# Another order of the helper calls in a four-engine graph network kernel on Trainium2

## The reference

```python
h = relu(layernorm(x)); A = (adj != 0)
for l in range(3):
    aggr = einsum('bst,bsd->btd', A, h @ weight[l])
    gi, gh = aggr @ w_ih.T + b_ih, h @ w_hh.T + b_hh
    r, z = sigmoid(gi_r + gh_r), sigmoid(gi_z + gh_z)
    h = (1 - z) * tanh(gi_n + r * gh_n) + z * h
x = x + h
hp = relu(layernorm(x)) @ W.T
e = leaky(hp @ a1 [rows] + hp @ a2 [columns], 0.2)
x = x + softmax(where(adj > 0, e, -9e15)) @ hp
```

## Time and profile before

| | us |
|---|---|
| median of 3 runs (498.48 to 499.28) | 499.28 |
| the profiled execution | 499.44 |
| its span, first to last instruction | 497.6 |
| PE, DVE, ACT, POOL busy in the span | 461.2, 442.6, 359.4, 142.5 |
| mean granted TensorE clock | 0.985 |

### The profile page before, as it was taken

How to read it: one execution, slowest core, us unless ns; L and a number is a source line. 1 busy time by engine, 2 the same in 40 slices (tenths; PEclk the granted TensorE clock), 3 DMA queues, 4 the chain that set the end, 5 groups by cost and what they waited for, 6 DMA issues and landing times.

```text
span 497.6 us, 8083 instructions
## 1 busy us (share of the span) xinstructions
PE 461.2 (93%) x2547; PEld 376.5 (76%) x2547; DVE 442.6 (89%) x1087; ACT 359.4 (72%) x641; POOL 142.5 (29%) x170
## 2 busy tenths in 40 slices
PE   5699998999999999999999999999999999998675
PEld 3476776887888878788888878788888888776465
DVE  3869888899999999999999999999999999997854
ACT  3365664786969778796968778795968878677375
POOL 2214244332312333332312333242213333131500
PEclk9989998999999999999999999999999999999979
DMA  6620030020303020030303021030303000000001
GB/s 179 211 85 2 1 105 0 20 89 22 107 21 107 22 86 22 22 106 21 107 23 106 12 69 49 22 106 23 105 22 106 1 24 1 22 1 22 23 1 42
DMA packets 26746, 26.34 MB, mean 53 GB/s; under 512 B 840, under 2 KB 18512, under 8 KB 26704
## 3 DMA queue, kind: packets, MB, share of 16 engines
q1 hardware_dynamic: 26704, 25.83, 16.2%
HBM read 21.63 MB, written 4.19 MB: 52 GB/s over the span
## 4 chain that ended last, share of the span: by engine, by line
PE 45%; DVE 27%; issue 13%; ACT 11%; DMA 2%; POOL 1%; SPq 1%; DVEq 0%; ACTq 0%; POOLq 0%
PE X L1108 12%; DVE prob L838 4%; DVE fresh L774 4%; DVE out_sb L850 4%; PE G L1193 3%; DVE neg_ring L706 3%; ACT e L455 3%; DVE rv L748 2%; PE R L1092 2%; PE R L1093 2%; PE R L1094 2%; PE Z L1092 2%; PE Z L1093 2%; PE G L1215 2%; PE Z L1094 2%
## 5 line engine op out<-in xcount | busy, mean ns | idle before, releaser
L1108 PE MATMUL X<-A_ring,nat_hi 128*128 128x512 f32 x192 | 78.8, 410 | 1.2 <-DVE A_ring L700 1.0
L1108 PE MATMUL X<-A_ring,nat_lo 128*128 128x512 f32 x192 | 76.3, 397 | 0.0
L838 DVE SCALAR_TENSOR_TENSOR prob<-e 128x512 f32<-128x512 f32 x64 | 62.0, 968 | 13.2 <-ACT e L456 13.0
L1226 PE MATMUL G<-hp,probT 128*128 128x128 f32 x512 | 67.3, 275 | 0.7 <-DVE out_sb L850 0.7
L275 POOL TENSOR_TENSOR hT_lo<-hT,hT_hi 128x512 fp32r<-128x512 f32 x19 | 25.4, 1337 | 147.6 <-ACT hT_hi L382 131.5
L1226 PEld LDWEIGHTS G<-hp,probT 128*128 128x128 f32 x512 | 63.2, 192 | 2.1 <-issue 0.9
L455 ACT ACTIVATE e<-g,nb 128x512 f32<-128x512 f32 x64 | 46.6, 729 | 5.6 <-DVE nb L831 5.5
L456 ACT ACTIVATE e<-g,nb 128x512 f32<-128x512 f32 x64 | 45.9, 717 | 0.0
L462 ACT COPY probT<-G 128x512 f32<-128x512 f32 x64 | 37.4, 584 | 10.4 <-PE G L1215 10.3
L432 ACT ACTIVATE gn<-npre,vecs 128x512 f32<-128x512 f32 x48 | 34.6, 720 | 13.7 <-DVE npre L758 13.7
L1108 PEld LDWEIGHTS X<-A_ring,nat_hi 128*128 128x128 f32 x192 | 36.5, 190 | 10.3 <-issue 1.6
(11 more groups left out here) (136 smaller groups left out, 1210.1 us busy)
## 6 DMA issues: line engine op xcount, KB each, us to landing
adj_raw<-in_adj SPq DMA_DIRECT2D x16, 1024.0 KB, 5.6
x_ring<-in_x SPq DMA_DIRECT2D x16, 256.0 KB, 2.9
out_x<-out_sb SPq DMA_DIRECT2D x16, 256.0 KB, 2.2
wih_in<-in_L_gnn_w_ih SPq DMA_DIRECT2D x1, 192.0 KB, 3.1
wl_in<-in_L_gnn_weight SPq DMA_DIRECT2D x1, 192.0 KB, 4.1
whh_in<-in_L_gnn_w_hh SPq DMA_DIRECT2D x1, 192.0 KB, 4.2
w_in<-in_L_gnn_W SPq DMA_DIRECT2D x1, 64.0 KB
vec_in<-in_L_gnn_b_ih SPq DMA_DIRECT2D x1, 1.5 KB
```

The costliest lines, as they stand in the source:

```text
L838: dve.scalar_tensor_tensor(out=prob[:, c], in0=e1[:, c % 2], scalar=1.0, in1=e2[:, c % 2], op0=ALU.mult, op1=ALU.max, accum_out=psums[:, k ...
L1108: mm = pe.matmul(X[:], part[s][:, c], A_ring[:, (k - s) % RING, c], start=(c == 0 and part is nat_hi), stop=(c == C - 1 and part is nat_lo))
L1226: mm = pe.matmul(G2[:, c * D:(c + 1) * D], probT[:, c % 2, j], hp[:, (k + 1) % 2, j, 0:D], start=(j == 0), stop=(j == C - 1))
```

## The change

The helpers and their instructions stay. Their sequence is another in rounds 0 to 3, in the repeated part and in rounds 16 to 19, on PE, ACT, DVE and POOL. The repeated part has its seam in another place: some calls of a round now stand at the head of the next one (`from_state(i - 1, 0, Z)` and `from_neighbours(i - 1, 0, Z)` on PE, `new_state(i - 1, 0)` on DVE, `state_high(i - 1, 1)` on ACT), and the statistics of x and `norm_scale` stand in the round before (`i + 1`). The new sequences, cut; those of before stand in the listing above:

```diff
 POOL
-            def full(i, k):
-                norm_scale(i, k)
-                natural_low0(i, k)
-                scale2(i, k)
-                centre2(i, k)
-                normed2(i, k)
-                state_low(i, k, 1)
+            def full(i):
+                natural_low0(i, i % RING)
+                scale2(i, i % RING)
+                centre2(i, i % RING)
+                normed2(i, i % RING)
+                norm_scale(i + 1, (i + 1) % RING)
+                state_low(i, i % RING, 1)
 ACT
+            def full(i):
+                neighbours_high(i, i % RING, 2)
+                own_candidate(i, i % RING, 2)
+                normed(i, i % RING)
+                state_high(i - 1, (i - 1) % RING, 1)
+                natural_high(i, i % RING, 1)
+                update_gate(i, i % RING, 2)
+                exps(i, i % RING, 0)
+                reset_gate(i, i % RING, 2)
+                neighbours_high(i, i % RING, 1)
+                exps(i, i % RING, 1)
+                turned_prob(i, i % RING, 0)
+                exps(i, i % RING, 2)
+                first_state_high(i, i % RING)
+                candidate(i, i % RING, 2)
+                turned_prob(i, i % RING, 1)
+                first_state(i, i % RING)
+                own_candidate(i, i % RING, 1)
+                exps(i, i % RING, 3)
+                reset_gate(i, i % RING, 1)
+                turned_prob(i, i % RING, 2)
+                neighbours_high(i, i % RING, 0)
+                turned_prob(i, i % RING, 3)
+                update_gate(i, i % RING, 1)
+                candidate(i, i % RING, 1)
+                attention_input(i, i % RING)
+                own_candidate(i, i % RING, 0)
+                reset_gate(i, i % RING, 0)
+                natural_high(i, i % RING, 2)
+                state_high(i, i % RING, 2)
+                values(i, i % RING)
+                update_gate(i, i % RING, 0)
+                candidate(i, i % RING, 0)
 DVE
+            def full(i):
+                new_state(i - 1, (i - 1) % RING, 0)
+                neighbours_low(i, i % RING, 2)
+                scores(i, i % RING)
+                natural_low(i, i % RING, 1)
+                offsets(i, i % RING)
+                adjacency(i, i % RING)
+                probabilities(i, i % RING, 0)
+                reset(i, i % RING, 2)
+                neighbours_low(i, i % RING, 1)
+                probabilities(i, i % RING, 1)
+                keep(i, i % RING, 2)
+                before_tanh(i, i % RING, 2)
+                probabilities(i, i % RING, 2)
+                natural_high0(i, i % RING)
+                residual(i, i % RING)
+                x2_stats(i, i % RING)
+                renew(i, i % RING, 2)
+                x2_mean(i, i % RING)
+                new_state(i, i % RING, 2)
+                state_low(i, i % RING, 0)
+                probabilities(i, i % RING, 3)
+                reset(i, i % RING, 1)
+                before_tanh(i, i % RING, 1)
+                neighbours_low(i, i % RING, 0)
+                x_stats(i + 1, (i + 1) % RING)
+                keep(i, i % RING, 1)
+                renew(i, i % RING, 1)
+                new_state(i, i % RING, 1)
+                output(i, i % RING)
+                mask(i, i % RING)
+                natural_low(i, i % RING, 2)
+                x_mean(i + 1, (i + 1) % RING)
+                reset(i, i % RING, 0)
+                before_tanh(i, i % RING, 0)
+                state_low(i, i % RING, 2)
+                keep(i, i % RING, 0)
+                renew(i, i % RING, 0)
 PE
+            def full(i):
+                from_state(i - 1, (i - 1) % RING, 0, Z)
+                from_neighbours(i - 1, (i - 1) % RING, 0, Z)
+                neighbours(i, i % RING, 2)
+                neighbour_terms(i, i % RING)
+                from_state(i, i % RING, 2, HN)
+                from_state(i, i % RING, 2, R)
+                from_state(i, i % RING, 2, Z)
+                from_neighbours(i, i % RING, 2, R)
+                turn_state(i, i % RING, 1)
+                from_neighbours(i, i % RING, 2, Z)
+                from_neighbours(i, i % RING, 2, IN)
+                turn_result(i, i % RING)
+                neighbours(i, i % RING, 1)
+                from_state(i, i % RING, 1, Z)
+                from_state(i, i % RING, 1, R)
+                turn_prob(i, i % RING, 0)
+                from_state(i, i % RING, 1, HN)
+                from_neighbours(i, i % RING, 1, Z)
+                turn_prob(i, i % RING, 1)
+                turn_input(i, i % RING)
+                attend(i, i % RING, 0)
+                from_neighbours(i, i % RING, 1, IN)
+                from_neighbours(i, i % RING, 1, R)
+                turn_prob(i, i % RING, 2)
+                attend(i, i % RING, 1)
+                neighbours(i, i % RING, 0)
+                turn_prob(i, i % RING, 3)
+                attend(i, i % RING, 2)
+                from_state(i, i % RING, 0, R)
+                from_state(i, i % RING, 0, HN)
+                turn_normed(i, i % RING)
+                attend(i, i % RING, 3)
+                from_neighbours(i, i % RING, 0, R)
+                turn_state(i, i % RING, 2)
+                from_neighbours(i, i % RING, 0, IN)
+                project(i, i % RING)
```

Of the written-out rounds, DVE's first calls and those of round 3, and POOL's of round 3:

```diff
             x_stats(0, 0)
             x_mean(0, 0)
             wl_out()
-            whh_out()
-            vectors_out()
-            natural_high0(0, 0)
-            whh_high()
             adjacency(0, 0)
+            natural_high0(0, 0)
+            x_stats(1, 1)
+            whh_out()
+            whh_high()
...
             neighbours_low(3, 3, 2)
             state_high(2, 2, 1)
-            x_mean(3, 3)
-            residual(3, 3)
             natural_low(3, 3, 1)
+            natural_high0(3, 3)
+            x2_stats(3, 3)
+            x2_mean(3, 3)
             reset(3, 3, 2)
             before_tanh(3, 3, 2)
-            x2_stats(3, 3)
-            x2_mean(3, 3)
             neighbours_low(3, 3, 1)
-            adjacency(3, 3)
-            natural_high0(3, 3)
             keep(3, 3, 2)
...
-            scale2(3, 3)
             natural_low0(3, 3)
             centre2(3, 3)
+            scale2(3, 3)
+            norm_scale(4, 0)
             normed2(3, 3)
```

More of the change, by code:

```diff
@@ L990, in _ @@
             natural_low(3, 3, 2)
+            mask(2, 2)
             keep(3, 3, 0)
@@ L994, in _ @@
             state_high(3, 3, 1)
-            every_graph(full)
+            neighbours_low(4, 0, 2)
+            scores(4, 0)
+            natural_low(4, 0, 1)
+            offsets(4, 0)
+            mask(3, 3)
+            adjacency(4, 0)
+            probabilities(4, 0, 0)
+            reset(4, 0, 2)
+            neighbours_low(4, 0, 1)
+            probabilities(4, 0, 1)
+            keep(4, 0, 2)
+            before_tanh(4, 0, 2)
+            probabilities(4, 0, 2)
+            natural_high0(4, 0)
@@ new lines, in _ @@
+            residual(4, 0)
+            x2_stats(4, 0)
+            renew(4, 0, 2)
+            x2_mean(4, 0)
+            new_state(4, 0, 2)
+            state_low(4, 0, 0)
+            probabilities(4, 0, 3)
+            reset(4, 0, 1)
+            before_tanh(4, 0, 1)
+            neighbours_low(4, 0, 0)
+            x_stats(5, 1)
+            keep(4, 0, 1)
+            renew(4, 0, 1)
+            new_state(4, 0, 1)
+            output(4, 0)
+            mask(4, 0)
+            natural_low(4, 0, 2)
@@ new lines, in _ @@
+            x_mean(5, 1)
+            reset(4, 0, 0)
+            before_tanh(4, 0, 0)
+            state_low(4, 0, 2)
+            keep(4, 0, 0)
+            renew(4, 0, 0)
+            for i in range(5, 15):
+                full(i)
+            new_state(14, 2, 0)
+            neighbours_low(15, 3, 2)
+            scores(15, 3)
+            natural_low(15, 3, 1)
+            offsets(15, 3)
+            adjacency(15, 3)
+            probabilities(15, 3, 0)
+            reset(15, 3, 2)
+            neighbours_low(15, 3, 1)
@@ new lines, in _ @@
+            probabilities(15, 3, 1)
+            keep(15, 3, 2)
+            before_tanh(15, 3, 2)
+            probabilities(15, 3, 2)
+            natural_high0(15, 3)
+            residual(15, 3)
+            x2_stats(15, 3)
+            renew(15, 3, 2)
+            x2_mean(15, 3)
+            new_state(15, 3, 2)
+            state_low(15, 3, 0)
+            probabilities(15, 3, 3)
+            reset(15, 3, 1)
+            before_tanh(15, 3, 1)
+            neighbours_low(15, 3, 0)
+            keep(15, 3, 1)
@@ L999, in _ @@
+            renew(15, 3, 1)
+            new_state(15, 3, 1)
+            output(15, 3)
+            mask(15, 3)
+            natural_low(15, 3, 2)
+            reset(15, 3, 0)
+            before_tanh(15, 3, 0)
+            state_low(15, 3, 2)
+            keep(15, 3, 0)
+            renew(15, 3, 0)
+            new_state(15, 3, 0)
+            neighbours_low(16, 0, 2)
             scores(16, 0)
             offsets(16, 0)
-            neighbours_low(16, 0, 2)
```

(20 more changed lines are left out.)

487 lines of the change are left out of this document (237 added, 250 removed).

## The result

| | before | after |
|---|---|---|
| median (range, executions) | 499.28 us (498.48 to 500.56, 4) | 481.28 us (479.26 to 482.75, 4) |
| ratio, with its 95% interval | | 0.9634 (0.9591 to 0.9678) |
| the profiled execution, its span | 499.44, 497.6 | 480.50, 478.7 |

The change makes the kernel 3.7% faster, 18 us; 484.0 had been forecast, and the range holds the result. From the page of the kernel after: the span, the busy times, the clock in 40 slices, the chain that ended last, and two groups of instructions (busy us in all and mean ns of one, then the idle time ahead and what ended it).

A forecast was written before the change was run, and what follows sets the result against it. Before, the loop of 28.2 us was taken to run through DVE, held by POOL; afterwards PE needs 27.1. 499.44 - 10.8 (rounds) - 3.5 (first graphs) - 1.0 (last graphs) = 484.1, forecast 484.0 us, range 479.5 to 494.

The forecast's parts named there:

- The twelve rounds: Repeated part, graph indices 4 to 15: each round falls from 28.2 to 27.3 us, -10.8 us (bounds -13.2 and -2.4).
- 0.2 us of waiting a round: PE in each new round: waiting added to its 27.1 us of work because the margins were thin, giving 27.3 us.
- the walk: One new round laid out step by step: every PE input ready first, DVE's own path 26.7 us against PE's 27.1.
- Before's loop runs through DVE: Rounds of the kernel before: holds and waits fill DVE to 28.2 us, its output is late, and PE waits.
- Subtract both: DVE in a round before: 28.2 less 0.95 of waits and 1.55 of holds leaves 25.7 us of work.
- First graphs: Rounds up to 3: round 3 saves 3.7 us, the first pass loses 1.7, later rounds regain; -3.5 (bounds -5 and +1).
- The first pass: Start of the launch: PE's first pass waits for the cast and POOL's nat_lo, starting at about 15.1 us, +1.7.
- Last graphs: Rounds 16 and 17: round 16 unchanged, fresh no longer held by h2n in 17; -1.0 us (bounds -2 and +1.5).
- New waits in place of the holds: First rival, in the rounds: late ACT instructions delay DVE, then PE; 27.9 us a round, 494 us; chance 0.22.
- Nothing: Third rival, in the rounds: another loop of 28.2 us lies behind the visible one; 496 to 500 us; chance 0.04.
- The slower one: Second rival: DVE makes POOL's x2c and h2n wait, turn_normed is late; round 29.05 us, 506.6 us; chance 0.12.
- the case in which both `x2c` and `h2n` lose every time: POOL in every new round: both issue second, turn_normed waits 0.4 us, about 489 us; chance within the first rival's.

The follow-up runs named there:

- experiment 1: Old order, and new order, each with POOL's three large instructions (nat_lo, x2c, h2n) cut to a quarter of their tile: 480.09 us old, 477.77 us new.
- experiment 6: New order with natural_high0 moved back ahead of the first probabilities in rounds 4 to 15: 485.99 us, ratio 0.9746 to the kernel before.
- (3): One more 512-wide DVE instruction a round ahead of residual, in both orders: old 499.78 us (ratio 1.0003), new 489.95 us (0.9799).
- (2): Four more transposes on PE in neighbour_terms, 0.44 us a round, in both orders: old 504.02 us (ratio 1.0100), new 485.81 us (0.9725).
- experiment 5: Old order with new order only in graphs 0 to 3: 494.86 us; in all but those: 485.63; in the last calls behind round 15: 496.34.

## Why the prediction was right, and where it was off

**The mechanism** (DVE is held when it reads two SBUF tiles beside large POOL instructions, and the new order parts them) is shown from three sides: with the holds taken away the old order has the whole gain of the rounds, and the stop of round 3 goes (experiment 1), one put back into the new order costs 0.55 us a round (6), and one moved by a pad goes to another instruction (3).

**The twelve rounds** were forecast at 27.3 us, "0.2 us of waiting a round", and came out at 27.07, the stated lower bound. Round by round that is 12 x (28.20 - 27.07) = 13.6 us instead of 10.8, and it is 2.8 of the 3.6 us between the sum (484.1) and the profiled execution (480.50). The sum of PE's steps, 27.1, was exact. The term that was off is the allowance of 0.2 us: in the walk every input was ready by 0.2 to 0.4 us, and in the trace PE waited for none. The margins are real, though, and thin: the walk's DVE waits were 0.3, 0.4 and 0.3 for `offsets`, and measured were 0.24, 0.38 and 0.12, with 0.27 ahead of the first `prob`, which the walk did not have; and 0.6 us more on DVE used up the 0.36 ahead of the fourth `turn_prob` (3).

**"Before's loop runs through DVE"** was wrong in its words and right in its sum. DVE alone did not set the pace: 0.44 us more on PE cost 0.32 a round (2), and 0.6 more on DVE cost nothing where it moved a hold away (3). "Subtract both", holds and waits, gave what DVE needs (25.7; it is marked busy 25.91 in the new round), not what the change would take away: the waits are still there after it and in experiment 1. That did no harm, because PE was the next limit at 27.1.

**First graphs**: -3.5 forecast, -4.0 in the traces, -3.3 (-2.1 to -4.6) in experiment 5. Round 3 was walked as 21.9 and took 22.02. Of its 3.55 us, 1.0 is the low clock behind the stop, by the same stop at a clock of 1.00 in experiment 5; the forecast had counted about 1.5 for it, from one execution. Not every execution of such an order has it, so that part of the agreement is luck. The first pass was put at 15.1 and came at 15.36, and behind its stop of 2.04 us the stretch from 16 to 20 has a clock of 0.57, 1.2 GHz for part of it. That was not foreseen; whether it belongs to the stop is open, since the kernel of experiment 6 has the same first calls, a stop of 2.71 us at 14.54, and 1.00 in that stretch.

**Last graphs**: -1.0 forecast; the end behind the middle pass of round 15 is 2.4 shorter, of which one round is 1.1, so -1.2. Experiment 5 has -1.8 for the two together, so -0.7 without the round.

**The rivals.** New waits in place of the holds: there are three on DVE, 0.89 us together, and none on PE. "Nothing": no. The slower one, POOL beaten to its start by DVE so that `turn_normed` waits: it does not happen in the profiled execution of the new order, where `h2n` is 1.04 us long in the rounds, but it happens in two of twelve rounds once DVE has 0.6 us more to do (3), for 1.8 us each, near the 1.95 that had been worked out, though most of it is one wait of PE for `h2n`, 1.23, and not the sum of small ones. Nothing here shows its chance of 0.12 as too high: the new order keeps its rounds only as long as a 128x4 instruction gets in at 237.13. By the rule of the Trainium skill, "SBUF — State Buffer", section "Who interferes with whom", whoever issues first has the shared port; the traces agree with that in both directions (POOL's 1.29 becomes 1.70, DVE's 0.69 becomes 1.77), and the case in which both `x2c` and `h2n` lose every time (489 us) did not come.

## What to carry to other kernels

Before reading an engine as full, look for instructions of one form with two durations, and for what the neighbour on the shared port does then: here two long `prob` out of four were worth the whole gain of the rounds. Waits of DVE for ACT stayed as they were and cost nothing once another engine set the pace, so ask of each wait whether it will still matter then. When every input of the pacing engine comes out ready in a walk, as here, forecast its own work with no allowance, and put the doubt into the range. A stage read from one trace each can be off by the clock of that execution; compare it with another kernel that has the same calls there. Do not take an engine's slack as room for an instruction: ask which meetings of DVE and POOL it shifts, and test such an order with one instruction more before trusting its margin.
